# Expert choice in an audio tower: the next pair's experts start four pieces later beside the spreading products, and the second list of rows is turned ten pieces sooner

## The reference

```python
logits = jnp.einsum('bsd,de->bse', x, gate_weight)
affinity = jax.nn.softmax(logits, axis=-1).transpose(0, 2, 1)
gating, index = jax.lax.top_k(affinity, k)
x_in = jnp.take_along_axis(x[:, None, :, :], index[..., None], axis=2)
h = jax.nn.gelu(jnp.einsum('bekd,edh->bekh', x_in, w1) + b1[None, :, None, :])
x_e = jnp.einsum('bekh,ehd->bekd', h, w2) + b2[None, :, None, :]
weighted = gating[..., None] * x_e
out = out.at[jnp.arange(Bx)[:, None], idx_flat].add(vals_flat)
```

## Time and profile before

| | us |
|---|---|
| median of 3 runs | 2271.65 |
| lowest, highest | 2266.53, 2272.15 |
| the profiled execution | 2271.49 |
| its span, first to last instruction | 2269.7 |
| TensorE busy in the span | 2015.7 |
| first spreading product to the end of the stage's last addition | 723.8 to 1041.1 |

### The profile page before, as it was taken

The page is one execution under the profiler, slowest core; times in us unless marked ns, Lnnn a source line. Parts: engine busy times, 40 slices in busy tenths (PEclk is TensorE's granted clock), DMA queues, the critical chain, the costliest instruction groups (busy, mean ns, idle before and its releaser), DMA issues. The chain is left out here.

```text
span 2269.7 us, 54561 instructions
## 1 busy us (share of the span) xinstructions
PE 2015.7 (89%) x20890; PEld 1786.3 (79%) x20890; DVE 1604.5 (71%) x4095; ACT 1071.8 (47%) x2699; POOL 602.3 (27%) x649
## 2 busy tenths in 40 slices
PE   6699999989746888996999999986999999999998
PEld 5488777779545787884777777766999999999998
DVE  4755555663583765665999999986777777777774
ACT  4433333332344565652676777753444444444443
POOL 0002222220005545520333334333212212221220
PEclk9699999999976999997999999997999999999999
DMA  8100000000221111100000000000000000000000
GB/s 186 43 1 12 11 12 11 11 11 1 67 59 40 41 34 40 40 22 1 3 3 3 3 3 3 3 3 1 8 14 7 7 7 14 7 7 14 7 8 15
DMA packets 80354, 44.50 MB, mean 20 GB/s; under 512 B 45800, under 2 KB 74024, under 8 KB 79752
## 3 DMA queue, kind: packets, MB, share of 16 engines
q1 hardware_dynamic: 74248, 29.53, 5.7%
q0 software_dynamic: 5888, 12.07, 2.0%
HBM read 27.20 MB, written 14.38 MB: 18 GB/s over the span
## 5 line engine op out<-in xcount | busy, mean ns | idle before, releaser
L2127 ACT ACTIVATE w<-banks,b 128x384 f32<-128x384 f32 (+1 forms) x512 | 259.3, 571 | 392.9 <-PE banks L2202 392.9
L2184 PE MATMUL banks<-w,w 128*128 128x128 f32 (+1 forms) x3072 | 364.1, 275 | 0.0
L2184 PEld LDWEIGHTS banks<-w,w 128*128 128x128 f32 (+1 forms) x3072 | 350.4, 189 | 9.1 <-issue 8.7
L1710 PE MATMUL banks<-qT,w 64*64 64x128 f32 (+1 forms) x4608 | 268.0, 269 | 13.2 <-DVE eb L1612 8.7
L1710 PEld LDWEIGHTS banks<-qT,w 64*64 64x64 f32 x4608 | 247.4, 134 | 31.0 <-issue 20.8
L1718 PE MATMUL banks<-eb,w 64*64 64x128 f32 (+1 forms) x4608 | 268.9, 270 | 1.0 <-DVE eb L1612 1.0
L1681 POOL TENSOR_TENSOR t<-eb 128x768 f32<-128x768 f32 x96 | 172.0, 1791 | 289.2 <-ACT eb L1658 286.6
L1718 PEld LDWEIGHTS banks<-eb,w 64*64 64x64 f32 x4608 | 244.1, 133 | 1.7 <-DVE eb L1612 1.5
L2024 DVE SCALAR_TENSOR_TENSOR h<-banks,t_wt,h 128x128 f32 (+3 forms) x672 | 183.5, 341 | 83.3 <-PE banks L2184 79.8
L1237 POOL DMA_INDIRECT xg<-xs,rowu x184 | 178.8, 972 | 127.5 <-DMA xg<-xs,rowu 83.6
L1612 DVE TENSOR_TENSOR eb<-eb,rd 128x1536 f32<-128x1536 f32 x96 | 210.8, 2196 | 2.3 <-ACT rd L1669 2.3
(11 more groups left out here) (305 smaller groups left out, 4261.3 us busy)
## 6 DMA issues: line engine op xcount, KB each, us to landing
out<-h SPq DMA_DIRECT2D x16, 320.0 KB
xs<-r_xl SPq DMA_DIRECT2D x16, 192.0 KB, 2.7
h<-in_xT SPq DMA_DIRECT2D x4, 750.0 KB, 14.9
h<-in_xT SPq DMA_DIRECT2D x4, 749.0 KB, 17.9
xg<-xs,rowu POOLq DMA_INDIRECT x184
xs<-r_xl SPq DMA_DIRECT2D x16, 128.0 KB
blocks<-NT SPq DMA_DIRECT2D x24, 48.0 KB, 1.9
D<-blocks SPq DMA_DIRECT2D x24, 48.0 KB, 2.0
```

What stands on the lines that cost most here:

```text
L1710: last = nc.tensor.matmul(lbanks(n)[place(n, hd), v, 0:wide(n)], k.Kt[half(hd), v, :], qT[half(hd), n // NC % 2, (n % NC) * P:(n % NC) * P ...
L2127: nc.scalar.activation(gb[u % 2][:, f, s * GW:s * GW + NFREE[s]], k.ps[:, order.bank(n), 0:NFREE[s]], ACT.Relu, bias=k.b1_1[:, 2 * e + f:2 ...
L2184: last = nc.tensor.matmul(k.psf[0:n, o:o + P], gb[u % 2][:, f, c * P:c * P + n], k.w2_1[:, 2 * e + f, :], start=(f == 0), stop=(f == 1))
```

## The change

The order is now built over all pieces of all pairs at once, with `LEAD = 4`. The unit n of the 24 shares of a front goes behind piece n+4 of the pair before (n-20 of its own pair for the last four shares), where it went behind piece n. In pair 0, pieces 0 to 3 stand between its last front units (outputs 11 to 15 and hidden 14 and 15). The turn of tiles 4 to 7 of a pair stands behind piece 0 of the pair, where it stood ahead of it. For each pair from 1 on the order around its start becomes: piece 23 of the pair before, hidden 13, piece 0, output 11, hidden 14, turn of tiles 4 to 7, piece 1, output 12, piece 2, addition, hidden 15, output 13, piece 3, outputs 14 and 15, turn of tiles 8 to 11, piece 4, addition, first gathered unit of the next pair. The last 20 pieces of pair 7 have no experts beside them, where it was 24. The order of the turns and additions among themselves, and so VectorE's queue, stays as it was. The second list is turned behind piece 8 of pair 2 in place of piece 18; its wait on bank 7 names the second half of batch 3's addition in place of batch 5's, and the wait of an addition for ScalarE's copies of the list moves from batch 5 to batch 4. No instruction's work changes and none is added.

```diff
     BATCHES = 6
+    LEAD = 4
...
     def units(self):
 
         out = []
-        for u in self.front():
-            out.append((0,) + u)
-            if u == ("output", max(self.experts_for(t) for t in range(4)) - 1):
-                out.append((0, "turned", 0))
-        pieces = self.pieces()
-        for p in range(PAIRS):
-            front, done = self.front() if p + 1 < PAIRS else [], 0
-            for n, (tile, par, lo, hi) in enumerate(pieces):
-                if lo == 0 and tile % 4 == 0:
+        pieces, front = self.pieces(), self.front()
+        N = len(pieces)
+        for at in range(self.LEAD - N, PAIRS * N):
+            if at >= 0:
+                p, n = divmod(at, N)
+                tile, par, lo, hi = pieces[n]
+                if n == 1:
+                    out.append((p, "turned", 1))
+                elif lo == 0 and tile and tile % 4 == 0:
                     if tile // 4 + 1 < self.BATCHES:
                         out.append((p, "turned", tile // 4 + 1))
                     elif p + 1 < PAIRS:
...
                 if n in (14, 16):
                     out.append((p, "added", (0, n // 2 - 7)))
-                if (p, n) == (2, 18):
+                if (p, n) == (2, 8):
                     out.append((p, "rows", 1))
-                upto = len(front) * (n + 1) // len(pieces)
-                out += [(p + 1,) + u for u in front[done:upto]]
-                done = upto
+            q, m = divmod(at + N - self.LEAD, N)
+            if q < PAIRS:
+                for u in front[len(front) * m // N:len(front) * (m + 1) // N]:
+                    out.append((q,) + u)
+                    if q == 0 and u == ("output", max(self.experts_for(t) for t in range(4)) - 1):
+                        out.append((0, "turned", 0))
         return out + [(PAIRS - 1, "added", (1, 0)), (PAIRS - 1, "added", (1, 1))]
...
                     if hf:
                         pe.wait_ge(row_moved, hf)
-                        pe.wait_ge(h_added, 2 * (2 * 2) + 2)
+                        pe.wait_ge(h_added, 2 * (2 * 1 + 1) + 2)
...
-                        if (b, s) in ((0, 0), (5, 0)):
+                        if (b, s) in ((0, 0), (4, 0)):
                             pe.wait_ge(row_moved, 1 if b == 0 else 2)
```

## The result

| | before | after |
|---|---|---|
| median of 19 runs each, us | 2270.21 | 2265.86 |
| lowest to highest | 2266.22 to 2272.15 | 2257.14 to 2271.82 |
| ratio, 95% interval | | 0.998, 0.9972 to 0.9989 |
| profiled execution, us | 2271.49 | 2265.05 |
| its span | 2269.7 | 2263.2 |

What follows compares the result with a forecast made beforehand. TensorE's in-order queue, 92% full in a quiet pair, was taken as the bound. -9.2 (pair 3) -3.9 (end) +9.9 (new order) = -3.2 us against 2271.49 gave 2268 us; 8 in 10 range 2258 to 2279.

Steps and rivals of the forecast that it cites:

- The term for pair 3: Second list turned ten pieces sooner: pair 3's waits for gathered rows and its slow clock go, -9.2 us.
- Pair 0, value 0: Four pieces fill idle time between pair 0's last expert products, but pair 1's gathers set the pace: no gain, 0.
- The end, -3.9 us: Last pair: four pieces fewer after the last expert product, and a shorter addition wait; -3.9 us, between -2.8 and -5.
- The new order, +9.9 us: Pair boundaries and middles: dependences with less work standing in them cost new waits, +9.9 us together, bounds 0 and +15.
- piece 23 to next piece 0: Pair boundary: ScalarE's copy between batches is less hidden, 0.70 us of waiting at seven boundaries, +4.9 us.
- output 11 to turn 4 to 7: Turn of tiles 4 to 7 now stands behind output 11 and one product: seven times 0.45, +3.2 us.
- output 15 to turn 8 to 11: Turn of tiles 8 to 11 directly behind output 15 takes 1.14 us instead of 0.39: 0.75 in six pairs, +4.5 us.
- The additions: First to second addition of even batches: the fifth gather's transposes between them shorten the wait for VectorE, -3.2 us.
- 1, no net cost: Rival: the new waits cost nothing net since ScalarE catches up in them; 2258.4 us, or halfway 2263; chance 0.24.
- 2, the clock falls at the pair ends: Rival: clustered waits before the turn of tiles 8 to 11 lower the clock; slower, 2280 or 2291 us; chance 0.13.
- 3, the gather queue: Rival: gathers become the bound from pair 4 on, some 1 us a pair, 2272 us; chance 0.06.
- 4, the list's move does nothing: Rival: the list's turn waits for the addition or its indices still come late, so 2277.5 us; chance 0.05.

Runs made afterwards that it cites:

- e2_lead: The changed kernel with the second list and its two waits put back behind piece 18 of pair 2; 2266.08 us, ratio 0.999.
- e7_gather_ahead: e5_smooth_add with GpSimd waiting for a group of gathers to land only after issuing the next group; 2224.03 us, ratio 0.9815.
- the second group: The changed kernel run again, unchanged, in another group of runs; 2265.97 us, ratio 0.9993.
- e3_turn: The changed kernel with output 15 behind piece 4 and the turn of tiles 8 to 11 after the next pair's first gathered unit; 2259.77 us, ratio 0.9967.
- e4_smooth: e3_turn with output 11 also moved ahead of piece 0 and hidden 5 ahead of piece 12; 2255.7 us, ratio 0.9952.
- e5_smooth_add: e4_smooth with the second addition of even batches behind piece 18 instead of 16; 2251.21 us, ratio 0.9945.
- e1_list: The kernel before with only the second list moved, from behind piece 18 to behind piece 8 of pair 2; 2260.41 us, ratio 0.9965.
- e8_last_only: e1_list with the last six front units of pair 7 moved behind its pieces 0 to 4; 2256.87 us, ratio 0.9957.

## Why the prediction was right

**The bound and the stall.** As read: TensorE's queue. The term for pair 3, -9.2 us, measured -7.9 (-10.0 to -5.7) alone, and its mechanism came as told: GpSimd no longer waits for the list. What the prediction didn't see is that the lead alone removes the same stall (e2_lead). It put the gain down to the list's move; in the sum this changes nothing, in a choice of what to keep it does.

**Pair 0, value 0.** Right, and for the reason given: from the first gathered transposes to pair 1's third, which waits for its gathers, it is 51.6 and 51.3 us in the two traces of before, 51.7 and 51.9 in those of after. The filled gaps bring nothing. The waits for xg are 4.3 us against 5.4. But that GpSimd's queue is full there holds only for this way of issuing: e7_gather_ahead takes that pair to 34.81 us with no wait for xg. The queue was not full of gathers but of waits for landings.

**The end, -3.9 us.** From output 15 to TensorE's last instruction 29.42 us became 24.01, so -5.4. The 2.8 and 0.8 came as counted. The other 1.7 or so is the clock: the wait for VectorE's addition is as long as before, and the clock no longer falls behind it. Busy time by stretch in the kernel after, where before 3.60 us ran at 0.53:

```profile
1026.00:1034.00 8.00, 6.08 (x37) 5.66 (x37) 5.19 (x16) 1.68 (x4) 0.00 (x0) 1.00 0.00 0
```

That wait, in the timeline of the kernel after:

```profile
1027.03 0.52 PE L1448 MATMUL banks<-ident,x_oT 128*128 128x128 f32 x3 [1.96 <-DVE h L1206]
```

It was 1.93 us before. The second traces agree: 29.43 us with a fall to 0.58, and 24.04 without. But the order is not what keeps the clock up. e2_lead has the same order there and the same gap, and its clock falls; its end takes 25.6 us, which is 3.85 under before, the counted value. The same stretch and that gap in e2_lead:

```profile
1026.00:1034.00 8.00, 6.04 (x29) 5.76 (x28) 7.54 (x22) 0.89 (x3) 0.00 (x0) 0.79 0.00 0
```

```profile
1029.30 0.52 PE L1448 MATMUL banks<-ident,x_oT 128*128 128x128 f32 x3 [1.96 <-DVE h L1206]
```

The same gap comes with and without a fall: the price of a gap was taken as fixed, and it isn't. What decides is open.

**The new order, +9.9 us.** By the steps, as start-to-start times in us for one (medians of the first traces; the second ones agree within 0.02):

| step | predicted | measured | times |
|---|---|---|---|
| piece 23 to next piece 0 | 0.70 | 0.36 to 1.14: 0.78 | 7 |
| piece 11 to 12 | 0.35 | 0.63 to 1.04: 0.41 | 6 |
| output 11 to turn 4 to 7 | 0.45 | 0.39 to 0.67: 0.28 | 7 |
| output 14 to 15 | -0.23 | 1.37 to 1.15: -0.22 | 7 |
| output 15 to turn 8 to 11 | 0.75 | 0.39 to 1.06: 0.67 | 6 |

Times their numbers, the predicted column sums to +13.1, the measured one to 5.46+2.46+1.96-1.54+4.02=+12.4. Output 11 to its turn was the most over-counted of these, 0.28 us and not 0.45. The additions are the term that was mis-sized most: -3.2 was expected. TensorE's wait for VectorE's addition over the stage fell from 7.7 and 8.5 us (two traces) to 5.4 and 7.5, 1.7 on the mean, and 0.8 of that is in the end already, so -0.9; the traces of one kernel differ by 2.1, so that size is rough. Start to start, the second addition behind piece 16 took 1.47 and 1.55 us (medians) and takes 1.38 and 1.48: 0.1 less each time, not 0.4. That VectorE itself was later by the rest is likely, since the transposes wait for it, but no run shows it.

**The sum.** -7.9 (or -9.2) -5.4 +12.4 -0.9 = -1.8 (or -3.1) us, where -3.2 was predicted, the medians give -4.3 (-6.4 to -2.5), the second group -1.6 and the stage in the traces -3.7. The large terms held by their own steps: the stall, the end's order and four of the five steps. That the sum came out so close is in part luck. The end gave 1.5 us more than counted, by a clock that another kernel with the same order doesn't keep, the steps cost 0.7 less, the stall gave 1.3 less and the additions 2.3 less, and these cancel. In the profiled executions the total fell by 6.4 us while the stage fell by 0.3: the rest lies in stages that the change doesn't touch, above all the attention's 487.4 us in that one trace, so one pair of traces would have told the wrong story of a right number.

**The rivals.** 1, no net cost: refuted. The whole change stands 3.4 us over the list alone by the ratios (5.6 by the medians and 6.4 by the ratios of the same group; the steps, the end and the additions give 6.1), and taking the waits away gives 3.0 (e3_turn, intervals overlap) and 6.4 us (e4_smooth) over after. A little of its "every wait lets it catch up" is true: e3_turn shows that the new waits stood in the place of one for VectorE's addition. 2, the clock falls at the pair ends: refuted, 10 us around each of the seven pair ends read 1.00 in both traces of after. The sign set for it, a clock by pair under 1.00, did show, but inside pairs: 0.96 in pair 2 of one trace and in pair 4 of the other, each behind a wait of over 1 us at piece 12 for ScalarE (1.13 and 1.68 us). By the Trainium skill's rule on short idle times between groups (page "TensorE: Matmul & The Clock Gate", section "A second HAM failure mode: psum-queue depth-cycling") the clock was to swing at the pair ends; these traces, with four waits in 8 us at each, don't agree. 3, the gather queue: not in after, but it appears as soon as pairs get shorter than its 38 us (e5_smooth_add). 4, the list's move does nothing: refuted alone by e1_list, yet true beside the lead.

**Signs that missed.** Quiet pairs were to take 39.5 us; they take 39.3 to 42.2 (39.9 to 43.4 in the second trace), more than the counted steps. The new waits at the turns, told as 0.4 and 0.6 to 0.8 us, are 0.20 and 0.51. Part of the excess comes with the unnamed waits of ScalarE, as at this piece 0, whose wait is 1.6 us long where the copy alone gives 0.7, in the timeline of the kernel after at pair 6's start:

```profile
965.31 0.58 PE L1432 MATMUL banks<-x_sel,x_yh 128*128 128x374 f32 x2 [1.59 <-ACT x_oT L1343]
```

## What to carry to other kernels

When work is taken out from between two dependent instructions, count each dependence by its start-to-start time with and without cover, not by the idle time shown, and put independent work back between them: here that turned a change worth some 4 us into one worth 11, of which ScalarE's fewer unnamed waits may be a part. Look for the wait that the removed one had hidden; here it took back 0.93 of 1.46 us a pair. Two edits that cure one stall are not worth the sum of both; run each alone before keeping the one that has a price. A queue that is "full" should be split into issuing and waiting for its own landings; here the waiting was the larger prize, but it must be measured on the very kernel that it is meant for, since it came with a gain of 27 us in one order of work and a loss of 71 and 84 in two others.

## What the runs showed of the hardware

- An indirect gather of 128 rows takes GpSimd 0.94 us and 0.30 to the next, 1.25 in all; waiting for each group of four to land adds 1.7 to 1.9 us in most groups (3.3 at most, in after), so that a group takes 6.5 us and not 5.0.
- ScalarE stands still for 1.5 to 13.6 us at a time, ended by nothing that the trace names, while gathers go out without a pause: over 10 us only in rows of 31 or more, up to 5.7 in rows of 12 to 20, in two kernels of three with that issue pattern. With a pause every four gathers the single waits are 0.5 to 2.6 us, partly at the same place of the program in two traces, and one such kernel, e8_last_only, has none. The cause is open.
- A wait of TensorE costs more than the idle time that the trace shows: 0.67 for 0.51, 0.78 for 0.66, 0.28 for 0.20 us, against the same step without a wait in before.
- The same gap of 1.9 us in the last pair was followed by 3.6 us at a clock of 0.53 and 0.58 in the two traces of before, by a fall in e2_lead (0.79 over the 8 us around it), and by none in two traces of after, whose order there is e2_lead's.
